# Each engine gets its own order of head steps in both layers, and the first layer's tail of y ends in the next pair

## The chip, the cores and the metric

The program runs on one core of a Trainium2 chip. That core has five engines that work side by side and meet only at semaphores: TensorE (PE, matrix products and transposes into PSUM), VectorE (DVE), ScalarE (ACT), GpSimd (POOL) and SyncE (SP, which here only issues DMA transfers). Each engine takes its own instructions strictly in the order in which they are written. An instruction whose semaphore is not there yet holds up everything behind it on its engine. The metric is the device time of one execution in microseconds (us).

## The reference, cut to what matters

```python
x = L0_attn_x                                    # (8, 256, 128)
for layer in (0, 1):
    xn = _layernorm(x)
    s = attn(xn)      # a selective scan over 256 tokens; 16 states (layer 0) or 2 x 16 chunks (layer 1)
    g = _silu(ffn(xn))  # 8 experts, 128 -> 512 -> 128; layer 0: one-hot choice, layer 1: a soft mixture
    x = x + s * g
# in attn, per state n:   h = exp(delta * A[n]) * h + delta * B[n] * xs;   y += h * C[n]
# layer 0 ends with       y = layernorm(y + x_res) * gamma + beta;  s = y @ W_out.T + b_out
# layer 1 ends with       y = (y + xs * Dskip) * silu(z);           s = y @ out_proj.T
```

All is fp32. The eight sequences are worked in four pairs (512 tokens each), all four through the first layer and then all four through the second, with the result of the first in a DRAM tensor `x1`.

## The kernel before

**Slots.** The work of a pair in a layer is written in 32 slots (`UNITS`), one for each of the 8 x 4 tiles of the experts' hidden layer. Every engine has its own function `slot0` (first layer) or `slot1` (second layer), which is called once per slot. So what stands in slot 7 on DVE and on PE is a statement about order, not about time: an engine that runs ahead is in a later slot than another at the same moment.

**A first-layer slot.** PE makes a hidden tile in three passes (L1413 to L1415, `three_passes`), ACT rectifies it (L1217), and PE multiplies the one of two slots ago by the down weights (L1470). Next to that run the 16 scan chunks, at the slots of `CHUNKS0` (0, 1, 2, 4, 5, 7, 8, 9, 11, 12, 14, 15, 16, 18, 19, 21): ACT makes the decay (L1204), DVE the drive (L652, from a row of B and C that a DMA spreads over the partitions into a ring of four tiles `CB`) and, a slot later, the scan (L659), POOL multiplies by C and adds up (L940 to L948), and PE sums groups of four into `Y_BANK` (L1434).

**A second-layer slot.** There are 32 chunks, almost one a slot, and PE has a gate tile (in pairs: the gates of two tiles in one slot), an up product (L1529) and a down product (L1538). There is one PSUM bank for the up product. `up` of a tile waits until DVE has multiplied the tile before it into `hid` (L775), and DVE waits for the up product. This ties PE and DVE together within about a slot.

**The head.** Before a pair's slots can start, its head has to be done: layer norm (`stat1`, `var1`, `xn`), the transpose `xnT`, the input products (`xin`, or `xi0`, `xi1`, `z0`, `z1`), the router (`logits`, `lmax`, `lexp`, then `pick`, `onehot` or `soft1` to `soft3`, `cwT`), the convolution (`tap1` to `tap3`, `xs`), the rows of B and C (`row`), and softplus (`dt`, `rest`, `less`, `ln`). The head of the next pair is spread over slots 6 (`LATE`) to 31 of the pair before. One table (`HEAD0` at L63, `HEAD1` at L66) says in which slot a step stands, **for all engines at once**. A step that needs several engines (`dt`: PE multiplies, ACT applies softplus) stands in the same slot on each. Nearly all head products go through one PSUM bank, `HEAD_BANK`. PE may write the next one only when the last has been read (`head_read`).

**The end of a pair.** In the first layer `TAIL0` (L85) closes y: add and transpose y in slot 27, its layer norm in 28 to 30, `ynT` and the product `s` in 31, all on the pair's own slots. What is left of the feed-forward result is in `late0`, in slots 0 to 5 of the next pair. DVE selects the last expert in slot 2, PE transposes into the head bank in slot 3 (L1517, L1518), ACT applies tanh in slot 3 (L1246), DVE multiplies in slots 4 and 5 (L718, L724), and POOL adds the residual (L979). The second layer has `late1` for the same: DVE adds y in slot 2 (L781), PE has both the transposes and the output product in slot 3, ACT tanh in 3 (L1289), DVE in 4 and 5.

**The queue of SP.** The DMAs stand in one program too. `send_rows` and `send_mask` write to DRAM and wait for the landing, and the loads of `CB` rows stand behind them.

## Time and profile before

| | before |
|---|---|
| median of 3 runs | 908.33 us (901.88 to 913.71) |
| the profiled execution | 906.77 us, of which 904.7 us are the span from first to last instruction |
| mean granted TensorE clock | 0.943 of full speed |
| busy: PE, DVE, ACT, POOL | 738.9, 631.9, 506.3, 527.0 us (82%, 70%, 56%, 58%) |
| longest waits of PE in total | 56.8 us in 44 waits of the up product for DVE's `hid`; 27.4 us in 4 waits of a transpose for DVE's `xn` |
| longest wait of ACT in total | 124.5 us in 87 waits for PE before a rectification |

No engine is full. One that waits is, most of the time, waiting in its own fixed order for something that another engine has in a later place of its own. A row of the timeline reads: start in us, length, engine, line, operation, out<-in, count, and in brackets the idle time of the engine before it with what ended it.

### The profile page before, as it was taken

How to read it: one execution, taken by the hardware profiler on the slowest of the kernel's cores; microseconds unless marked ns; L12 is line 12 of the kernel's file. 1: busy time of each engine (PE TensorE's matmuls, PEld its weight loads, DVE VectorE, ACT ScalarE, POOL GpSimd, SP SyncE). 2: the span in 40 equal slices, each digit the busy share in tenths (PEclk: the TensorE clock that was granted, in tenths of full speed). 3: DMA queues.
4: the chain of work that ended last, by engine and by line, in shares of the span. 5: the costliest groups of instructions: out<-in, count | busy, mean ns of one | idle time of the engine just before them, and what ended most of it. 6: DMA issues, size and time to landing. Idle time of an engine off the chain costs nothing. (4 is left out here: it accounts for less than half of the span.)

```text
span 904.7 us, 8892 instructions
## 1 busy us (share of the span) xinstructions
PE 738.9 (82%) x2160; PEld 392.1 (43%) x2160; DVE 631.9 (70%) x1013; ACT 506.3 (56%) x755; POOL 527.0 (58%) x420
## 2 busy tenths in 40 slices
PE   2747987899789967868799769898778896888996
PEld 1324554455445543434444335453344442344443
DVE  4399559936984765357776578766669676778884
ACT  2734544455446535676646557557557456656661
POOL 0086526534661563208856658866659765659894
PEclk9988988998899989989999999999889999999999
DMA  9275465443734583267735467747456655648881
GB/s 269 74 214 153 124 221 144 137 140 98 181 97 132 153 227 90 76 155 185 200 106 150 123 161 182 190 124 175 119 146 179 183 143 124 152 125 214 203 192 34
DMA packets 90515, 137.86 MB, mean 152 GB/s; under 512 B 7896, under 2 KB 29088, under 8 KB 90464
## 3 DMA queue, kind: packets, MB, share of 16 engines
q1 hardware_dynamic: 90464, 137.30, 57.1%
q8 instruction: 17, 0.28, 0.1%
q14 instruction: 34, 0.28, 0.1%
HBM read 133.73 MB, written 3.54 MB: 152 GB/s over the span
## 5 line engine op out<-in xcount | busy, mean ns | idle before, releaser
L659 DVE TENSOR_TENSOR_SCAN state<-decay,bank 128x512 f32<-128x512 f32 x192 | 233.7, 1217 | 11.7 <-ACT decay L1204 1.0
L1413 PE MATMUL bank<-XH,wh 128*128 128x512 f32 x256 | 170.9, 667 | 26.7 <-ACT sg L1253 12.8
L1529 PE MATMUL bank<-xw,wu 128*128 128x512 f32 x256 | 141.5, 635 | 57.1 <-DVE hid L775 56.8
L923 POOL TENSOR_TENSOR product<-state,CB 128x512 f32<-128x512 f32 x96 | 122.4, 1275 | 86.4 <-DVE state L659 84.6
L1217 ACT ACTIVATE hid<-bank,early 128x512 f32<-128x512 f32 x128 | 86.9, 684 | 132.7 <-PE bank L1470 124.5
L652 DVE TENSOR_TENSOR bank<-bank,CB 128x512 f32<-128x512 f32 x192 | 133.5, 695 | 27.9 <-DMA CB<-crow 20.7
L1470 PE MATMUL bank<-hid,wd 128*128 128x512 f32 x256 | 143.6, 644 | 0.0
L1204 ACT ACTIVATE decay<-delta,negA 128x510 f32<-128x510 f32 x192 | 126.9, 710 | 10.0 <-DVE delta L639 7.3
L1538 PE MATMUL bank<-hid,wd 128*128 128x512 f32 x256 | 132.2, 599 | 0.0
L925 POOL TENSOR_TENSOR product<-product 128x512 f32<-128x512 f32 x96 | 123.6, 1288 | 7.5
L1253 ACT ACTIVATE sg<-bank 128x512 f32<-128x512 f32 x128 | 74.3, 597 | 89.2 <-PE bank L1415 81.0
L775 DVE TENSOR_TENSOR hid<-sg,bank 128x512 f32<-128x512 f32 x128 | 85.9, 671 | 54.0 <-PE bank L1529 49.3
L1414 PE MATMUL bank<-XL,wh 128*128 128x512 f32 x256 | 107.2, 419 | 0.0
L1415 PE MATMUL bank<-XH,wl 128*128 128x512 f32 x256 | 106.8, 417 | 0.0
L1529 PEld LDWEIGHTS bank<-xw,wu 128*128 128x128 f32 x256 | 44.5, 194 | 139.4 <-DVE hid L775 85.9
L944 POOL TENSOR_TENSOR product<-state,CB 128x512 f32<-128x512 f32 x48 | 61.4, 1280 | 72.0 <-DVE state L659 69.8
L1413 PEld LDWEIGHTS bank<-XH,wh 128*128 128x128 f32 x256 | 51.9, 203 | 88.0 <-issue 37.2
L1414 PEld LDWEIGHTS bank<-XL,wh 128*128 128x128 f32 x256 | 52.2, 204 | 38.4 <-issue 35.1
L948 POOL TENSOR_TENSOR product<-product 128x512 f32<-128x512 f32 x48 | 62.8, 1307 | 3.8
L1538 PEld LDWEIGHTS bank<-hid,wd 128*128 128x128 f32 x256 | 47.9, 191 | 37.0 <-issue 30.7
L992 POOL TENSOR_TENSOR xw<-XR,cwb 128x512 f32<-128x512 f32 x32 | 42.1, 1316 | 30.5 <-DVE wl L529 13.7
L919 POOL TENSOR_TENSOR product<-state,CB 128x512 f32<-128x512 f32 x32 | 40.9, 1277 | 31.1 <-DVE state L659 17.8
(166 smaller groups left out, 922.3 us busy)
## 6 DMA issues: line engine op xcount, KB each, us to landing
CB<-crow SPq DMA_DIRECT2D x256, 256.0 KB, 5.1
CB<-crow SPq DMA_DIRECT2D x64, 512.0 KB, 5.4
cwb<-cwrow SPq DMA_DIRECT2D x64, 256.0 KB, 5.6
wu<-W_dram SPq DMA_DIRECT2D x8, 256.0 KB, 5.9
wd<-W_dram SPq DMA_DIRECT2D x8, 256.0 KB, 5.9
wu<-Wu_dram SPq DMA_DIRECT2D x8, 256.0 KB, 5.6
xw<-Wg_dram SPq DMA_DIRECT2D x8, 256.0 KB, 4.1
wd<-Wd_dram SPq DMA_DIRECT2D x8, 256.0 KB, 4.3
```

The costliest lines, as they stand in the source:

```text
L652: v.tensor_tensor(drive, dx, CB[:, c % ROWS, 1, :], ALU.mult).then_inc(drive_ready.sem, 1)
L659: v.tensor_tensor_scan(state[:, c % RING, :], decay[:, PLACE[c], :], drive, 0.0, ALU.mult, ALU.add).then_inc(state_ready.sem, 1)
L923: p.tensor_tensor(addend, state[:, c % RING, :], cs, ALU.mult).then_inc(state_used.sem, 1)
L925: ins = p.tensor_tensor(product[:, e % PRODS, :], product[:, e % PRODS, :], addend, ALU.add)
L1204: a.activation(by_batch(decay[:, PLACE[c], :])[:, :, 1:], by_batch(delta[:, m, :])[:, :, 1:], ACT.Exp, scale=negA[:, c:c + 1]).then_inc(de ...
L1217: a.activation(hid[:, u % 2, :], bank[HID_BANK + u % HIDS][:, :], ACT.Relu, bias=col0("b1", u)).then_inc(hid_ready.sem, 1)
L1413: t.matmul(dst, wh[:, e, ws], XH[:, :], start=True, stop=False)
L1414: t.matmul(dst, wh[:, e, ws], XL[:, :], start=False, stop=False)
L1415: return t.matmul(dst, wl[:, e, ws], XH[:, :], start=False, stop=stop)
L1470: t.matmul(bank[out_bank(e)][:, :], wd[:, u, :], hid[:, u % 2, :], start=(f == 0), stop=(f == FT - 1)).then_inc(down_done.sem, 1)
L1529: t.matmul(bank[UP_BANK][:, :], wu[:, e, 128 * f:128 * f + 128], xw[:, e % 2, :], start=True, stop=True).then_inc(up_ps.sem, 1)
L1538: ins = t.matmul(bank[OUT_BANK][:, :], wd[:, u, :], hid[:, u % 2, :], start=(u == 0), stop=(u == UNITS - 1))
```

## The change

**Own orders.** For the heads that run beside another pair of the same layer, the common tables give way to one table per engine: `PE0`, `ACT0`, `DVE0`, `POOL0` for the first layer and `PE1`, `ACT1`, `DVE1`, `POOL1` for the second. A reader of something stands a slot or more behind its maker in nearly all places (in the second layer PE's `dt0` stands in slot 17, and it needs the head bank free of `cwT`, which ACT reads in slot 17 too). The heads start at slot 1 instead of 6: DVE has `xn` in slot 4 where it was in 9, PE has `xnT` in 7 where it was in 11. The loads of x move ahead for that. `HEAD0` and `HEAD1` remain for the very first head and for the head of the second layer's first pair, which runs in the last pair of the first layer. Their numbers change too: the `z0`, `z1` steps move from 16 and 20 to 23 and 25, and `onehot` goes to the end of the first head.

```diff
-HEAD0 = {6: "stat1", 7: "var1", 9: "xn", 10: "stat2", 11: "xnT var2", 12: "xin", 13: "logits xf tap1", 14: "lmax tap2",
+PE0 = {7: "xnT", 9: "xin", 11: "logits", 13: "xfT", 15: "z", 18: "dt", 20: "row", 22: "onehot"}
+DVE0 = {1: "stat1", 2: "var1", 4: "xn", 5: "stat2", 7: "var2", 9: "xf", 11: "tap1", 12: "lmax tap2", 13: "tap3", 14: "prob",
+        15: "pick", 16: "xs", 17: "zx", 22: "rest"}
+EXTRA = {3: "xi0", 4: "xi1", 5: "z0", 6: "z1"}
+PE1 = {6: "xnT", 8: "logits", 9: "xi0a", 10: "xi0b", 13: "row0 xi1a", 14: "xi1b", 15: "cwT", 17: "dt0", 18: "z0",
+       21: "row1", 22: "z1", 23: "dt1"}
...
-FINISH_Y0 = CHUNKS1[N - 1] + SUM_LAG1
-
-TAIL0 = {27: "y", 28: "yn1", 29: "yn2", 30: "yn", 31: "ynT s"}
+FINISH_Y0 = CHUNKS1[N - 1] + SUM_LAG1 + 1
+
+DVE_TAIL0 = {27: "y", 29: "yn1 yn2", 31: "yn"}
+PE_TAIL0 = {28: "y"}
+DVE_LATE0 = {1: "ynT", 3: "s"}
+PE_LATE0 = {0: "yn", 2: "s"}
...
+STREAM = [item for e in range(E) for item in ([EXTRA[e]] if e in EXTRA else []) + list(range(FT * e, FT * e + FT))]
+def stream_bank(item):
+
+    return HID_BANK + STREAM.index(item) % HIDS
...
+            def gate_at(i):
+
+                return 4 if i == PAIRS - 1 else 6
...
-                v.tensor_scalar(ynT, dx, col0("gam"), col0("bet"), ALU.mult, ALU.add).then_inc(ynT_ready.sem, 1)
+                    v.tensor_scalar(ynT, bank[Y_BANK][:, :], col0("gam"), col0("bet"), ALU.mult, ALU.add).then_inc(ynT_ready.sem, 1)
...
-                if u == 2:
+                if u == 3:
                     finish_y(i, 1)
 
-                if u == 4:
+                if u == 5:
                     dve.wait_ge(tg_ready.sem, tg_ready.at1(i, 1))
...
+            load_x(1, 0)
+            send_rows(0, 0, 0)
             send_mask(0)
-            send_rows(0, 0, 0)
```

**The extras of the second layer.** `xi0`, `xi1`, `z0`, `z1` no longer pass through the head bank. Each takes a place in the stream of gate tiles through the two `HID` banks, ahead of expert 3, 4, 5, 6. ACT reads it just before the four gate tiles of that expert. Round these places PE writes one gate tile in one slot and three in the next, where it was two and two. The four products of `xi` are written in two halves.

**The tails.** In the first layer the transposes of yn, `ynT`, and the product `s` move to slots 0 to 3 of the next pair, and go through `Y_BANK` alone. DVE's two steps of the gate move from slots 4 and 5 to 6 and 7 (`gate_at`), in another buffer. In the second layer DVE adds the end of y in slot 3 instead of 2. The output product and tanh are in slot 4 instead of 3, DVE's product in 5 instead of 4.

On DVE, in the first layer, at the start of the second pair, before: `L718` is the first step of the gate of the pair before (`yfT`), `L724` the second.

```order
L652 TENSOR_TENSOR bank<-bank,CB 128x512
L659 SCALAR_TENSOR_TENSOR state<-decay,bank 128x512
L718 SCALAR_TENSOR_TENSOR yfT<-yfT,bank 128x512
L652 TENSOR_TENSOR bank<-bank,CB 128x512
L659 SCALAR_TENSOR_TENSOR state<-decay,bank 128x512
L724 SCALAR_TENSOR_TENSOR so<-yfT,hp,so 128x128 x4
L652 TENSOR_TENSOR bank<-bank,CB 128x512
L659 SCALAR_TENSOR_TENSOR state<-decay,bank 128x512
L631 MEMSET pause 128x1
L632 COPY_PREDICATED yfT<-cwb,bank 128x512
L682 COPY szm<-ohT 8x512
```

The same place now, from the third scan on. `L782` and `L788` are the gate's two steps, `L602` is `xn` of the next pair, `L738` the end of `s`.

```order
L714 SCALAR_TENSOR_TENSOR state<-decay,bank 128x512
L738 TENSOR_TENSOR so<-bank,bout 128x512
L707 TENSOR_TENSOR bank<-bank,CB 128x512
L602 TENSOR_SCALAR xn<-xt,mv,rstd 128x128 x4
L714 SCALAR_TENSOR_TENSOR state<-decay,bank 128x512
L707 TENSOR_TENSOR bank<-bank,CB 128x512
L589 BN_STATS stats<-xn 128x6 x4
L714 SCALAR_TENSOR_TENSOR state<-decay,bank 128x512
L782 SCALAR_TENSOR_TENSOR sg<-sg,bank 128x512
L686 MEMSET pause 128x1
L687 COPY_PREDICATED yfT<-cwb,bank 128x512
L788 SCALAR_TENSOR_TENSOR so<-sg,hp,so 128x128 x4
```

The gate moved behind two more scans, and `xn` of the next pair now stands ahead of it.

On DVE, in the second layer, at the start of the second pair, before: `L781` adds the end of y, which needs the last sum of PE, and the scan of the new pair stands behind it.

```order
L659 SCALAR_TENSOR_TENSOR state<-decay,bank 128x512
L652 TENSOR_TENSOR bank<-bank,CB 128x512
L781 TENSOR_TENSOR xd<-xd,bank 128x512
L785 TENSOR_TENSOR xd<-xd,szm 128x512
L659 SCALAR_TENSOR_TENSOR state<-decay,bank 128x512
L775 TENSOR_TENSOR hid<-sg,bank 128x512
```

Now, where the same two steps are `L845` and `L849`:

```order
L714 SCALAR_TENSOR_TENSOR state<-decay,bank 128x512
L839 TENSOR_TENSOR hid<-sg,bank 128x512
L707 TENSOR_TENSOR bank<-bank,CB 128x512
L593 MEMSET idle 128x1
L595 BN_AGGR mv<-stats 128x2 x4
L597 TENSOR_SCALAR veps<-mv 128x4
L845 TENSOR_TENSOR xd<-xd,bank 128x512
L849 TENSOR_TENSOR xd<-xd,szm 128x512
L714 SCALAR_TENSOR_TENSOR state<-decay,bank 128x512
```

The end of y moved one scan and one `hid` back.

On ACT, in the second layer, where the router's weights `cwT` and softplus of `dt0` stand now (second pair, slots 16 to 19): `L1206` is the extra, `L1319` are four gate tiles, `L1267` four decays, `L1222` is `cwT`, `L1146` on is `dt0`.

```order
L1206 ACT_TABLE_LOAD
L1206 ACTIVATE xs<-bank,early 128x512
L1319 ACTIVATE sg<-bank 128x512 x4
L1267 ACT_TABLE_LOAD
L1267 ACTIVATE decay<-delta,negA 128x2x255 x4
L1222 ACTIVATE ohT<-bank 8x512
L1146 ACTIVATE sp_e<-bank,early 128x512
L1147 ACTIVATE sp_x<-bank,early 128x512
```

Before, `cwT` (L1159) was the last of these steps, behind both softplus steps:

```order
L1253 ACTIVATE sg<-bank 128x512 x4
L1204 ACT_TABLE_LOAD
L1204 ACTIVATE decay<-delta,negA 128x2x255 x4
L1083 ACTIVATE sp_e<-bank,early 128x512
L1084 ACTIVATE sp_x<-bank,early 128x512
L1085 ACTIVATE sp_e<-sp_e 128x512
L1087 ACTIVATE sp_u<-sp_e 128x512
L1159 ACTIVATE ohT<-bank 8x512
```

`cwT` moved from behind the second softplus to ahead of the first.

## Rows read from the trace of the kernel before

**Rows 1.** Busy time by pair: stretch, length, PE, PEld, DVE, ACT, POOL, PEclk, DMA share, GB/s

```profile
27.50:121.20 93.70, 71.77 (x218) 40.24 (x217) 66.94 (x121) 51.98 (x82) 45.88 (x37) 0.93 0.56 169
121.20:206.30 85.10, 72.41 (x229) 42.19 (x228) 62.45 (x119) 43.52 (x70) 42.01 (x33) 0.90 0.49 136
291.40:395.00 103.60, 80.80 (x247) 44.54 (x246) 57.01 (x103) 58.78 (x95) 41.39 (x33) 0.92 0.47 130
395.00:527.80 132.80, 112.60 (x310) 55.93 (x308) 93.80 (x131) 79.06 (x115) 87.75 (x69) 0.95 0.63 164
527.80:656.80 129.00, 109.66 (x312) 55.38 (x312) 93.99 (x130) 79.21 (x114) 89.26 (x70) 0.96 0.61 152
```

**Rows 2.** Timeline of PE in the first layer's second pair: rows with a wait

```profile
153.03 1.09 PE L1338 MATMUL bank<-early,xn 128*128 128x128 f32 x4 [5.48 <-DVE xn L547]
...
165.72 0.66 PE L1338 MATMUL bank<-early,sg 128*128 128x128 f32 x4 [1.56 <-DVE lg L592]
...
173.66 0.58 PE L1367 MATMUL bank<-early,onehot 128*8 128x128 f32 x2 [2.60 <-DVE onehot L599]
```

**Rows 3.** Timeline of DVE, first layer: the gate's wait, and xn there and at the start

```profile
134.33 0.69 DVE L718 SCALAR_TENSOR_TENSOR yfT<-yfT,bank 128x512 f32<-128x512 f32 x1 [5.92 <-ACT yfT L1246]
...
149.81 3.08 DVE L547 TENSOR_SCALAR xn<-xt,mv,rstd 128x128 f32<-128x128 f32 x4
```

**Rows 4.** Timeline of DVE at the very start, with POOL idle

```profile
9.54 1.12 DVE L547 TENSOR_SCALAR xn<-xt,mv,rstd 128x128 f32<-128x128 f32 x4 [4.54 <-POOL rstd L890]
```

**Rows 5.** Busy time of the second pair up to DVE's zx (columns as in rows 1)

```profile
121.20:180.90 59.70, 48.70 (x148) 28.54 (x147) 51.32 (x91) 28.84 (x48) 34.60 (x27) 0.86 0.51 139
```

**Rows 6.** The page's costliest groups: DVE's scan and drive

```profile
L659 DVE TENSOR_TENSOR_SCAN state<-decay,bank 128x512 f32<-128x512 f32 x192 | 233.7, 1217 | 11.7 <-ACT decay L1204 1.0
...
L652 DVE TENSOR_TENSOR bank<-bank,CB 128x512 f32<-128x512 f32 x192 | 133.5, 695 | 27.9 <-DMA CB<-crow 20.7
```

**Rows 7.** Timeline of PE in the first layer's last pair: rows with a wait

```profile
323.46 1.09 PE L1338 MATMUL bank<-early,xn 128*128 128x128 f32 x4 [7.24 <-ACT xn L1132]
...
343.32 1.19 PE L1343 MATMUL bank<-XNP,later 128*128 128x512 f32 x2 [3.59 <-ACT xs L1143]
...
394.21 1.16 PE L1494 MATMUL bank<-later,xd 128*128 128x128 f32 x8 [3.97 <-DVE xd L703]
```

**Rows 8.** Timeline of PE in the second layer's second pair: rows with a wait

```profile
541.05 1.13 PE L1529 MATMUL bank<-xw,wu 128*128 128x512 f32 x2 [3.76 <-DVE hid L775]
...
577.34 0.50 PE L1413 MATMUL bank<-XH,wh 128*128 128x512 f32 x1 [2.60 <-ACT sg L1253]
...
618.24 1.13 PE L1529 MATMUL bank<-xw,wu 128*128 128x512 f32 x2 [1.45 <-DVE hid L775]
...
625.86 0.50 PE L1413 MATMUL bank<-XH,wh 128*128 128x512 f32 x1 [1.27 <-ACT sg L1253]
...
637.38 2.07 PE L1529 MATMUL bank<-xw,wu 128*128 128x512 f32 x2 [4.05 <-DVE hid L775]
...
652.59 1.12 PE L1529 MATMUL bank<-xw,wu 128*128 128x512 f32 x2 [1.84 <-DVE hid L775]
```

**Rows 9.** Timeline of ACT and DVE there: what these waits hang on

```profile
574.78 0.60 ACT L1138 ACTIVATE XNP<-bank 128x512 f32<-128x512 f32 x1 [5.58 <-PE bank L1338]
...
634.92 0.69 DVE L563 SCALAR_TENSOR_TENSOR sp_e<-sp_u,sp_e 128x512 f32<-128x512 f32 x1 [4.34 <-ACT sp_u L1087]
```

**Rows 10.** Busy time round the longest wait and round the pair's start

```profile
626.00:640.00 14.00, 9.93 (x21) 4.11 (x22) 8.20 (x11) 7.85 (x12) 9.16 (x8) 0.80 0.59 125
524.40:546.10 21.70, 15.54 (x47) 8.98 (x47) 15.43 (x18) 9.81 (x15) 11.96 (x10) 0.92 0.53 138
```

**Rows 11.** Timeline of ACT and SP at the start: before the first CB rows

```profile
39.49 0.20 ACT L1115 ACTIVATE warm<-ones 128x1 f32<-128x1 f32 x1
...
38.07 2.87 SPq L371 DMA_DIRECT2D CB<-crow  x4
```

**Rows 12.** Waits of SP's queue: total, times, longest

```profile
SPq L412 <- ACT ohT L1159: 41.2, 4, 11.5
```

336 lines of the change are left out of this document (199 added, 137 removed).

## Prediction

> **What bounds the kernel now.** First the busy time by pair [rows 1]. The reader sees two kinds of pairs. A first-layer pair takes 85.1 us, in which PE is busy for 72.4 and DVE for 62.5. The first pair takes 93.7, the third is like the second, and the last takes 103.6, since it carries the second layer's head. A second-layer pair with a head beside it takes 129.0 to 132.8 us, with PE at 110 to 113, DVE at 94 and POOL at 88 to 89. PE is thus nearest to a bound in both layers, but 12.7 us of the first kind and 19.3 us of the second are idle on PE. Its work does not change, so what can be won is this idle time, and what the clock loses round it (granted 0.90 and 0.96).
>
> Then the timeline of PE, only the rows that have a wait. In the first layer a pair has three that count: 5.48 us for `xn`, 1.56 for the router's `lmax`, 2.60 for `onehot` [rows 2]. All are head steps, where PE stands in the same slot as, or close behind, a DVE step that is late. DVE is late because it sat still itself for 5.92 us, for ACT's tanh of the old pair's gate, before its fourth scan [rows 3]. In the second layer there are the 3.76 us at the pair's start and then 2.60, 1.45, 1.27, 4.05 and 1.84, together 11.2 [rows 8]. ACT and DVE show what stands behind two of them: ACT waits 5.58 us for `xnT` with four gate tiles queued behind it, and DVE waits 4.34 us in `rest1` for ACT's softplus with the scan and the next `hid` queued behind [rows 9]. Both are waits of a reader that stands in its maker's slot.
>
> **The change, first layer.** No instruction is added but for the split of `xi`, and no pass is removed. The sum is one of places. Take a middle pair (85.1 us) in two parts.
>
> Up to `zx`, which the next `dt` product of PE waits for, DVE should set the pace: the old stretch is 59.7 us long with 51.3 of DVE work [rows 5], so 8.4 idle. In the new order `zx` stands in slot 17 and no more in 20. Two scans (1.22 each), two drives (0.70 each) and a select (taken as a drive) now come after it [rows 6], 4.5 us less. `ynT` and `s` come in from the pair before, at about a drive each, 1.4 us more. That leaves 48.2 us of work. The 5.92 us wait falls: the gate is behind two more scans and PE's transposes, which ACT waits for, are long done. `xn` for PE's slot 7 is made in DVE's slot 4. I put 2 us for what DVE still waits (short gaps of dependent instructions), so `dt` can start some 50 us into the pair. Before it PE will wait anew: by this count DVE needs more than PE for slots 8 to 12, so about 4 us for `lmax` (PE slot 13, DVE slot 12) and 2 us for `zx`. These waits are in the 50.
>
> From there to the end PE sets the pace. The old stretch from `onehot` (slot 18, at 173.66) to the pair's end at 206.3 is 32.6 us [rows 1, 2]. `z` leaves it (1.2 us, by the like product) and so does `s` (1.2 us) [rows 7]. Some 1.5 us more go, because the clock stays up with the 2.60 us wait gone and because the yn transposes no longer wait in slot 31. That makes 28.7. The pair takes 79 us, 6 less. Twice: 12.
>
> Here price and place of `xn` matter. At 149.81 its four pieces took 3.08 us beside POOL's products [rows 3], at the very start, with POOL idle, 1.12 us [rows 4]. In slot 4 POOL has chunk 2 in hand, so I keep 3.08; `xf` is the same form. The Trainium skill (SBUF — State Buffer, Who interferes with whom) says why: VectorE and GpSimd share one pair of SBUF ports as an exclusive lock, and whoever comes second blocks for the whole instruction. By the start's row both steps together would cost 4 us less and the pair 75; by that rule, as by the row beside POOL, 79.
>
> The first pair gains the same kind of waits, but pays at the start. `CB` rows could be loaded from 38.07 on, once the rows of B and C were out. Now `send_mask` stands ahead of the loads, and its `onehot` is copied by ACT behind the warm-up at 39.49 [rows 11]. Bounds: 1.6 us if the rest hides, about 5 with the copy and a landed write; a shorter first head gives back about one. I take 3 later. Gain 6 less 3: 3 us.
>
> The last first-layer pair: 7.24 us for `xn`, 3.59 for `xs0` ahead of `z0`, 3.97 for `ynT` ahead of `s` [rows 7], 14.8 in all. `xnT` stays in slot 11, but DVE no longer sits 5.9 us before it; 5 of 7.2 fall. The `z` wait falls, since z is now 7 slots behind `xs0`; a new one of about 2 us comes in slot 24, where `row1` needs the bank that ACT reads only after softplus. `ynT` is gone from this place. 5 + 3.6 - 2 + 3.4 = 10.
>
> First layer: 3 + 12 + 10 = 25 us.
>
> **The change, second layer.** At a pair's start, DVE's end of y needs PE's last sum, and the scan stands behind it. One slot later it should find the sum ready: the 3.76 us fall. The stretch round it ran at 0.92 of the clock [rows 10], 1.7 us lost at 21.7 us, of which I count 1.4. So 5.2 at each of three starts.
>
> In the slots of a head: the five waits of 11.2 us fall as they stand, and so does a loss of clock (0.80 over 14 us with PE busy 9.9 [rows 10]), 2 us. In their place come new ones. (a) PE's `dt0` in slot 17 needs `cwT` read by ACT in slot 17, and there ACT has an extra, four gate tiles, a table load and four decays ahead of it. (b) Three gate tiles in one slot instead of two, four times: the third waits for ACT. (c) `xs1` waits for DVE's `dx` of slot 15, and a gate tile waits for `xs1`. (d) SP's three blocking sends now lie within slots 14 to 22. No row shows these waits. Below they cost nothing; above, I bound them by the 11.2 us that they replace. I take 7, nearer to the upper end, since (a) is exactly the pattern of what is removed, and (b) to (d) are of one or two us each. So a head stretch gains 11.2 + 2 - 7 = 6.2. First pair: 6.2, less the 1.2 us of `s`, the waits of the first layer's tail in its slots 0 to 5, and a smaller loss of clock: 3. Second and third: 6.2 + 5.2 = 11.4 each. Last: 5.2. Second layer: 31 us.
>
> **Sum.** 906.8 - 25 - 31 = 851 us, against the profiled execution's own 906.77. That is 1.6 us below the median of the runs, 908.33, so I leave it as it is.
>
> **Rivals.** (1) The new waits are small: nothing in the second layer's (a) to (d), and DVE's and PE's parts of a first-layer pair overlap better. 21 us back there, some 6 in the first layer: about 824 us. For it speaks that the waits left on PE would then be those of the ties between `up` and `hid`.
> (2) The waits only move, half. DVE fills the first layer (62.5 of then 79 us), and its head steps meet POOL more often, each for up to 2 us more [rows 3, 4]; in the second layer (a) to (d) cost all of the 11.2. 4 x 3 + 3 x 4.2 + some 2: 878 us. The port lock of the Trainium skill is the rule that speaks for this.
> (3) The waits move one for one: PE and DVE are tied within a slot, and what is taken from one slot is waited for in the next. Only the starts (3 x 3.8) stay won: 895 us. Against it: the removed waits have a named cause, a reader in its maker's slot.
> (4) Slower: SP's queue. The `CB` loads stand behind `row0`, `cwT`, `row1`, now in slots 14, 17 and 22. A wait of SP for ACT's `cwT` reached 11.5 us [rows 12]. If each of the nine held the scans for 9 us, 81 us would be lost against 56 won: about 932 us. It decides from (56 + 18) / 9 = 8.2 us each. Against it: the ring holds four rows, and DVE waited for `CB` only 20.7 us over the whole run [rows 6].
>
> **How the numbers follow.** The forecast (836 to 868) 0.52; (1) 0.12; (2) 0.17; (3) 0.14; (4) 0.05. The predicted time is that of the forecast. The range 818 to 886 takes in the forecast, (1) and (2), 0.81. A measurement of this kernel, whose three runs lie 1.3% apart, can tell about 2% (890 us) from no change. Faster by over 2%: 0.81; within 2%: 0.14; slower: 0.05.
>
> **What would show it.** In the changed profile: first-layer middle pairs of 77 to 81 us. DVE's gate step without an idle time ahead of it, and `xnT` with less than 2 us. PE waits for `lmax` and for `zx` that are longer than before. Second-layer pairs of 116 to 119 us, no wait over 2 us in the up product at the start, and a wait of about 2 us before `dt0`. `CB` rows first loaded at about 41 us. The prediction is wrong if DVE waits for `CB` rows for far more than 20.7 us, if DVE's `xn` or `xf` takes over 3.1 us, or if PE's idle time in a second-layer pair stays above 16 us.

## The result, and the profile after

The changed kernel took 851.6 us (median of 4 runs, 845.5 to 853.8) beside 906.0 us (901.9 to 913.7) of the kernel before: a ratio of 0.938, 95% interval 0.930 to 0.947. The forecast was 851 us with a range of 818 to 886. The total was met almost to the microsecond, but not because each term was: several were wrong by 2 to 11 us and cancelled. The rest of this text is about that.

| | after |
|---|---|
| the profiled execution | 845.54 us, span 843.1 us |
| mean granted TensorE clock | 0.965 |
| busy: PE, DVE, ACT, POOL | 722.5, 618.1, 507.6, 531.0 us (86%, 73%, 60%, 63%) |
| longest waits of PE in total | 27.2 us (was 56.8) of the up product for DVE's `hid` |
| longest wait of ACT in total | 110.8 us (was 124.5) before a rectification |

The busy time by pair of the changed kernel answers [rows 1]. Columns: stretch, length, PE, PEld, DVE, ACT, POOL, PEclk, DMA share, GB/s.

```profile
27.50:120.50 93.00, 73.91 (x214) 40.68 (x214) 64.61 (x119) 52.12 (x83) 46.82 (x37) 0.89 0.57 168
120.50:196.60 76.10, 65.65 (x229) 38.35 (x228) 60.49 (x119) 42.87 (x70) 42.76 (x33) 1.00 0.54 151
196.60:272.90 76.30, 68.89 (x230) 40.19 (x229) 60.73 (x119) 43.13 (x71) 42.78 (x33) 0.96 0.52 149
272.90:373.70 100.80, 82.31 (x253) 46.23 (x252) 56.30 (x108) 62.39 (x98) 42.70 (x34) 0.92 0.51 144
373.70:490.70 117.00, 105.99 (x305) 53.19 (x305) 90.42 (x130) 79.53 (x116) 85.59 (x68) 0.98 0.68 176
490.70:610.80 120.10, 110.25 (x313) 55.08 (x312) 92.33 (x129) 79.28 (x113) 89.55 (x71) 0.97 0.65 167
610.80:729.80 119.00, 108.74 (x313) 53.96 (x312) 92.76 (x129) 79.27 (x114) 89.59 (x71) 0.99 0.63 166
729.80:843.10 113.30, 99.04 (x291) 49.96 (x289) 88.56 (x110) 61.78 (x84) 88.95 (x70) 1.00 0.64 159
sum 815.60, PE 714.78 PEld 377.63 DVE 606.21 ACT 500.38 POOL 528.74; mean PE 89.35 PEld 47.20 DVE 75.78 ACT 62.55 POOL 66.09
```

The cuts are at ACT's first rectification or Silu of a pair. Read at the same marks, the kernel before has pairs of 93.6, 85.2, 85.1, 107.0, 131.1, 128.9, 130.6 and 115.8 us (its fourth pair is longer here than in [rows 1], whose cuts lay a little earlier). So the eight pairs gained 0.7, 9.0, 8.9, 6.2, 14.0, 8.8, 11.6 and 2.5 us: 24.8 in the first layer (forecast 25) and 36.9 in the second (forecast 31).

What of this is idle time and what is clock? The same sum for the kernel before, by layer:

```profile
27.60:398.40 370.80, 300.96 (x925) 170.83 (x925) 251.45 (x463) 199.04 (x316) 172.23 (x137) 0.91 0.51 143
398.40:904.70 506.30, 429.07 (x1211) 215.70 (x1210) 368.48 (x493) 299.29 (x425) 352.51 (x278) 0.97 0.61 156
```

PE was idle for 877.1 - 730.0 = 147.1 us of this and is now idle for 815.6 - 714.8 = 100.8: 46.3 us less. In the other 15.2 us PE is busy for less: the same products in less time, at a higher granted clock (0.94 and 0.98 of full by layer, 0.91 and 0.97 before; 5.1 of the 15.2 lie in the second layer).

The two waits that the prediction expected to grow in a first-layer pair are the first two rows of the timeline of PE (second pair); the next two are the places foreseen in the second layer (sixth pair):

```profile
154.56 0.66 PE L1398 MATMUL bank<-early,sg 128*128 128x128 f32 x4 [3.80 <-DVE lg L647]
...
167.60 0.70 PE L1403 MATMUL bank<-xs,early 128*128 128x512 f32 x1 [2.87 <-DVE xs L670]
...
507.04 1.49 PE L1635 MATMUL bank<-xw,wu 128*128 128x512 f32 x2 [1.92 <-DVE hid L839]
...
562.78 1.12 PE L1403 MATMUL bank<-rows,w_dt 32*128 32x512 f32 x2 [1.34 <-ACT ohT L1222]
...
599.40 0.50 PE L1505 MATMUL bank<-XH,wh 128*128 128x512 f32 x1 [2.22 <-ACT sg L1319]
```

`lmax` 3.80 us (forecast 4), `zx` 2.87 (forecast 2), the longest wait at the start of the sixth pair 1.92 (forecast: none over 2), and `dt0` 1.34 (forecast 2). The last one, 2.22 us before a gate tile, was in no list.

And DVE up to `zx`, where the prediction said that it sets the pace (columns as above; the second row is the rest of the pair):

```profile
120.50:167.50 47.00, 38.34 (x138) 22.57 (x136) 45.31 (x88) 26.47 (x45) 31.70 (x25) 1.00 0.61 169
167.50:196.60 29.10, 27.31 (x91) 15.78 (x92) 15.18 (x34) 16.41 (x25) 11.07 (x9) 1.00 0.42 122
```

DVE works 45.3 of 47.0 us. The stretch was forecast at some 50, the rest at 28.7.

Cut at the start of `zx` itself, and not behind it, the same two parts can be read in every kernel, also in those of the experiments below. "Clock" is the granted clock, "2" and "3" the second and third pair (us):

```text
kernel and pair      up to zx  clock    rest  clock
before, 2                59.1   0.86    26.0   1.00
after, 2                 46.4   1.00    29.7   1.00
after, 3                 46.5   0.93    29.8   1.00
after, again, 3          46.4   0.93    31.3   0.95
cb_first, 2              46.4   0.93    32.7   0.90
gate_early, 2            50.6   0.87    29.8   1.00
gate_early, 3            49.7   0.90    29.8   1.00
tail_in_pair, 2          47.4   0.89    32.9   0.95
tail_in_pair, 3          46.0   0.93    32.7   0.95
head0_old, 2             53.0   0.97    23.4   1.00
same_slot0, 2            44.3   0.96    30.6   1.00
```

Up to `zx` the length does not follow the clock: 46.4 us at 1.00 and at 0.93. Behind it, it does: 29.7 us at 1.00, 31.3 at 0.95, 32.7 at 0.90 (the edit of `cb_first` does not touch this pair). That bears out the prediction's two parts, DVE's and then PE's. It also shows that the 12.7 us won ahead of `zx` are not the clock's: with the gate undone the stretch ran at 0.87, nearly as low as before, and took 50.6 us, not 59.1. Four of these rows as the profile gives them (`gate_early`, `tail_in_pair`, `cb_first`, the second execution):

```profile
121.30:171.90 50.60, 41.92 (x138) 25.09 (x136) 45.48 (x85) 25.38 (x43) 31.12 (x24) 0.87 0.58 155
...
171.30:204.20 32.90, 30.15 (x99) 17.52 (x100) 16.89 (x37) 16.44 (x26) 11.30 (x10) 0.95 0.36 111
...
162.90:195.60 32.70, 30.26 (x91) 17.37 (x92) 14.97 (x35) 16.40 (x25) 11.32 (x10) 0.90 0.38 113
...
244.10:275.40 31.30, 28.92 (x91) 16.64 (x92) 15.64 (x35) 16.44 (x26) 11.25 (x10) 0.95 0.43 126
```

### The profile page after: what moved, and what is told of

It is laid out like the page before. It is cut to its first block and busy times, and to the rows that moved or that the text cites. A ratio compares the mean times of both kernels' runs of the same rounds, so it can differ in the third digit from the quotient of the medians.

```text
span 843.1 us, 8895 instructions
## 1 busy us (share of the span) xinstructions
PE 722.5 (86%) x2160; PEld 382.7 (45%) x2160; DVE 618.1 (73%) x1013; ACT 507.6 (60%) x757; POOL 531.0 (63%) x420
## 5 line engine op out<-in xcount | busy, mean ns | idle before, releaser
L714 DVE TENSOR_TENSOR_SCAN state<-decay,bank 128x512 f32<-128x512 f32 x192 | 233.7, 1217 | 11.3 <-ACT decay L1267 0.9
L1505 PE MATMUL bank<-XH,wh 128*128 128x512 f32 x256 | 172.3, 673 | 26.3 <-ACT hid L1280 10.9
L1635 PE MATMUL bank<-xw,wu 128*128 128x512 f32 x256 | 137.6, 619 | 27.5 <-DVE hid L839 27.2
L1280 ACT ACTIVATE hid<-bank,early 128x512 f32<-128x512 f32 x128 | 86.9, 684 | 119.8 <-PE bank L1568 110.8
L707 DVE TENSOR_TENSOR bank<-bank,CB 128x512 f32<-128x512 f32 x192 | 133.4, 695 | 26.4 <-DMA CB<-crow 18.9
L1319 ACT ACTIVATE sg<-bank 128x512 f32<-128x512 f32 x128 | 75.4, 597 | 104.3 <-PE bank L1507 94.7
L839 DVE TENSOR_TENSOR hid<-sg,bank 128x512 f32<-128x512 f32 x128 | 85.9, 671 | 64.8 <-PE bank L1635 61.5
L1267 ACT ACTIVATE decay<-delta,negA 128x510 f32<-128x510 f32 x192 | 126.9, 710 | 8.0 <-DVE state L714 4.5
L987 POOL TENSOR_TENSOR product<-product 128x512 f32<-128x512 f32 x96 | 124.2, 1293 | 7.5
L1506 PE MATMUL bank<-XL,wh 128*128 128x512 f32 x256 | 105.1, 411 | 0.0
L1010 POOL TENSOR_TENSOR product<-product 128x512 f32<-128x512 f32 x48 | 65.0, 1354 | 3.8
L1057 POOL TENSOR_TENSOR xw<-XR,cwb 128x512 f32<-128x512 f32 x32 | 42.1, 1315 | 25.1 <-DMA cwb<-cwrow 20.7
```

What stands on the lines that cost most here:

```text
L707: v.tensor_tensor(drive, dx, CB[:, c % ROWS, 1, :], ALU.mult).then_inc(drive_ready.sem, 1)
L714: v.tensor_tensor_scan(state[:, c % RING, :], decay[:, PLACE[c], :], drive, 0.0, ALU.mult, ALU.add).then_inc(state_ready.sem, 1)
L987: ins = p.tensor_tensor(product[:, e % PRODS, :], product[:, e % PRODS, :], addend, ALU.add)
L1267: a.activation(by_batch(decay[:, PLACE[c], :])[:, :, 1:], by_batch(delta[:, m, :])[:, :, 1:], ACT.Exp, scale=negA[:, c:c + 1]).then_inc(de ...
L1280: a.activation(hid[:, u % 2, :], bank[HID_BANK + u % HIDS][:, :], ACT.Relu, bias=col0("b1", u)).then_inc(hid_ready.sem, 1)
L1505: t.matmul(dst, wh[:, e, ws], XH[:, :], start=True, stop=False)
```

## The experiments

All start from the changed kernel. Most were timed once only, and one time differs from the next by up to 1%, so the verdicts rest on the length of pairs in the trace, cut at the same marks. This table has them all (us):

```text
pair                   1      2      3      4      5      6      7      8    span
before               93.6   85.2   85.1  107.0  131.1  128.9  130.6  115.8   904.7
after                92.9   76.2   76.2  100.8  117.0  120.1  119.0  113.3   843.1
after, again         93.9   76.2   77.7  102.1  116.8  120.1  119.3  114.6   848.4
gate_early           93.8   80.4   79.4  105.7  116.8  122.8  120.1  114.9   861.3
tail_in_pair         96.4   80.3   78.7  101.6  119.8  119.1  119.0  114.7   857.1
head0_old            93.9   76.4   76.2  100.8  120.8  120.4  118.9  115.0   849.8
same_slot0           93.3   75.0   74.9  102.0  120.0  120.1  119.5  114.6   846.9
same_slot1           93.1   76.2   76.2  100.8  122.7  126.2  126.9  113.3   862.9
l2_start             93.4   76.2   77.6  102.0  117.3  122.5  122.3  119.4   858.4
cb_first             89.0   79.1   76.2   99.0  117.5  119.2  119.2  114.7   841.3
tail_first           94.1   76.2   76.2   94.5  123.1  120.6  118.8  115.2   846.2
tail_cb1             93.8   76.2   76.2   95.0  118.8  120.3  118.7  112.9   839.3
two_steps            94.2   76.2   76.2  100.8  117.9  119.8  118.7  114.6   846.0
together             87.8   74.9   74.9   97.8  117.7  119.2  122.9  115.1   837.9
```

### How sharp a pair is

> The changed kernel as it is, once more, to see how far the length of a pair differs between two profiled executions of one program. If a pair is a sharp measure, the eight lengths are 92.9, 76.2, 76.2, 100.8, 117.0, 120.1, 119.0 and 113.3 us again, each within 0.5 us. If the clock's low stretches fall at other places each time, single pairs differ by 1 to 3 us, and only sums of several pairs can be read.

No edit. It took 850.3 us. Single pairs differ by up to 1.5 us, and PE's idle time over all pairs was 100.7 against 100.8 us. In the second layer it repeats pair by pair, within 0.4 us. In the first it repeats only in sum: the first pair had 2.1 us more of it, the second 3.0 less, and the second was as long as before. So a difference under 1.5 us in one pair is no verdict, unless it returns in others. The fifth pair is the worst mark: it was 3.0 to 4.0 us longer in two kernels whose edits cannot reach it (same_slot0, head0_old) while its idle time was 11.3 and 10.5 us, as in the changed kernel (11.0).

### The gate step back in slot 4

```diff
         def gate_at(i):
-            return 4 if i == PAIRS - 1 else 6
+            return 4
```

> The gate step of the pair before is back in slot 4 for every pair, where it was; the head steps and the tail of y keep their new places. Theory of the prediction: VectorE's wait of 5.9 us for ScalarE's tanh was what made the head of the next pair late, so moving it removes most of a middle pair's gain. The wait comes back with 4 to 6 us, and the second and third pair take 80 to 82 us instead of 76.2; the other pairs stay. Rival: the gain comes from the early start of the head's statistics (slots 1 to 5), and the gate step has slack in either place. Then the wait comes back, but the pairs take at most 77.5 us.

863.3 us. The timeline of DVE (the gate) and of PE (the product behind `lmax`) in the second pair:

```profile
135.14 0.69 DVE L782 SCALAR_TENSOR_TENSOR sg<-sg,bank 128x512 f32<-128x512 f32 x1 [3.56 <-ACT sg L1312]
...
159.59 1.12 PE L1398 MATMUL bank<-early,sg 128*128 128x128 f32 x4 [7.03 <-DVE lg L647]
```

In the changed kernel the gate step stands at 137.37 with no idle time ahead of it, and PE waits 3.80 (2.81 in the second execution). Here DVE waits 3.56 us, PE's wait grows to 7.03 us, and the second, third and fourth pair take 4.2, 1.7 to 3.2 and 3.6 to 4.9 us more (the fourth holds the gate of the third). The whole of it lies ahead of `zx`, where the clock does not count: 50.6 and 49.7 us instead of 46.4 in the second and third pair, and the rest is unchanged. The theory holds, a little below its size: 3.2 to 4.2 of a middle pair's 9 us hang on one instruction's slot, on the engine that sets the pace.

### The tail of y back in its own pair

```diff
-DVE_TAIL0 = {27: "y", 29: "yn1 yn2", 31: "yn"}
-PE_TAIL0 = {28: "y"}
-DVE_LATE0 = {1: "ynT", 3: "s"}
-PE_LATE0 = {0: "yn", 2: "s"}
+DVE_TAIL0 = {27: "y", 28: "yn1", 29: "yn2", 30: "yn", 31: "ynT s"}
+PE_TAIL0 = {27: "y", 30: "yn", 31: "s"}
+DVE_LATE0 = {}
+PE_LATE0 = {}
```

> The tail of y of a first-layer pair (slots 27 to 31 on VectorE and TensorE) ends again within the pair; the head steps and the gate keep their new places. Theory of the prediction: the tail cost a middle pair 1.4 us of VectorE's slots either way, and at the last first-layer pair 3.4 us of waiting in slot 31. So the second and third pair stay within 1 us of 76.2 (77.7 at most, by the clock's stretches), and the fourth takes 3 to 4 us more than 100.8 to 102.1. Rival: the tail in the pair is a chain TensorE, VectorE, TensorE, VectorE in five slots whose waits stop both engines in every pair. Then the second and third pair take 3 us or more longer too.

858.9 us. Here the prediction's own account fell on both counts. The first pair takes 2.5 to 3.5 us more, the second 4.0, the third 1.0 to 2.5; the fourth, where it saw 3.4 us, is unchanged. What the tail takes in a middle pair is seen in DVE's waits at the boundary:

```profile
190.24 0.69 DVE L722 TENSOR_TENSOR xd<-XR,bank 128x512 f32<-128x512 f32 x1 [1.58 <-PE bank L1526]
...
193.41 0.89 DVE L589 BATCH_NORM_STATS2 stats<-bank 128x6 f32<-128x128 f32 x4 [2.49 <-PE bank L1398]
...
196.62 0.06 DVE L686 MEMSET pause<- 128x1 f32 x1 [1.69 <-PE bank L1568]
...
201.82 0.69 DVE L738 TENSOR_TENSOR so<-bank,bout 128x512 f32<-128x512 f32 x1 [1.65 <-PE bank L1581]
```

These are turns between DVE and PE, one after the other, and the next pair's first scan stands behind them on DVE. In the changed kernel the waits of 4.0 us before the statistics and 1.6 before `y` are as long or longer, but `ynT` and `s` no longer stand between the pair's end and the next scan. At the last first-layer pair PE's waits become 4.76 us for `y`, 0.62 for `yn` and 3.97 for `s` (as [rows 7]), 9.4 together, where the changed kernel has 3.20 and 5.62, 8.8 together: the tail costs about the same there in both orders.

Not all of the 4.0 and 2.5 us is the tail's. Behind `zx` the two pairs take 32.9 and 32.7 us, 3 more than in the changed kernel, but at a granted clock of 0.95, and a pair with the new tail took 31.3 there at the same clock. So with the clock taken off, the tail costs 2.6 us in the second pair and 1.0 in the third. Whether its waits also bring the lower clock is not shown.

### The first layer's head in its old slots

```diff
+HEAD0 = {6: "stat1", 7: "var1", 9: "xn", 10: "stat2", 11: "xnT var2", 12: "xin", 13: "logits xf tap1", 14: "lmax tap2",
+         15: "lexp xfT tap3", 16: "th pick", 17: "xs prob", 18: "onehot", 19: "z", 20: "zx", 22: "dt", 23: "row", 24: "rest",
+         25: "less ln"}
+PE0 = ACT0 = DVE0 = POOL0 = HEAD0
...
-FIRST = steps(HEAD0)[:steps(HEAD0).index("z")]
-BETWEEN = {0: "z zx", 1: "dt", 2: "row rest", 3: "less ln onehot"}
+FIRST = steps(HEAD0)[:steps(HEAD0).index("onehot") + 1]
+BETWEEN = {0: "z zx", 1: "dt", 2: "row rest", 3: "less ln"}
...
+            send_mask(0)
             send_rows(0, 0, 0)
-            send_mask(0)
...
-                    if u == LATE and i + 2 < PAIRS:
+                    if u == LATE + 4 and i + 2 < PAIRS:
                         load_x(i + 2, 0)
```

> The first layer's head has its old slots and one order for all engines (xnT 11, onehot 18, z 19, dt 22), also ahead of the first pair; gate step and tail of y keep their new places. A middle pair went from 85.1 to 76.2 us. Putting the gate back alone gave 79.4 and 80.4, the tail alone 78.7 and 80.3. Theory: the three parts add up, and the early head is worth what is left, 1.5 to 3 us, so the second and third pair take 78 to 80 us. Rival A: the head's new places carry most of the gain (the waits for lmax, xs and onehot), and the pairs take 81 to 84 us. Rival B: gate and tail matter only because the early head needs the slots that they left; with the old head their new places are enough by themselves, and the pairs take under 77.5 us.

851.9 us, and the second and third pair take 76.4 and 76.2 us, as with the new tables. Rival B is right. With the gate and the tail in their new places, `PE0`, `ACT0`, `DVE0` and `POOL0` add nothing to a middle pair. No run takes gate and tail back together, so it is not shown that these two make the whole 9 us. The old `xn` wait, 5.48 us in [rows 2], is down to 1.80 without the head having moved, since DVE does not sit still before it. Timeline of PE, second pair:

```profile
146.89 0.63 PE L1394 MATMUL bank<-early,xn 128*128 128x128 f32 x4 [1.80 <-DVE xn L598]
...
159.83 0.66 PE L1394 MATMUL bank<-early,sg 128*128 128x128 f32 x4 [3.44 <-DVE lg L643]
```

The sum shows why the places don't matter. Here `zx` comes at 174.4, in slot 20, and the stretch from 121.4 to 174.0 is 52.6 us long with 49.4 of DVE work. In the changed kernel `zx` starts 46.4 us into the pair, here 53.0. But PE has the one-hot behind it by then, and the rest of the pair is 23.5 us here and 29.8 there. What leaves DVE's part joins PE's.

The first pair is another matter. This kernel issues its first rows at 38.17 us, as early as the kernel before (38.07), and still takes 93.9 us there, while a kernel with the new tables and the rows at 37.40 takes 89.0 (`cb_first`, below). So in that pair up to 4.9 us hang on the new tables or on the new order of the very first head. The two were not tried apart.

### Readers a slot earlier, first layer

```diff
-ACT0 = {8: "xnT", 10: "xin", 13: "lexp", 14: "xfT th", 19: "dt", 21: "row", 23: "onehot", 24: "ln"}
-DVE0 = {..., 11: "tap1", 12: "lmax tap2", 13: "tap3", 14: "prob", 15: "pick", 16: "xs", 17: "zx", 22: "rest"}
-POOL0 = {2: "var1", 7: "var2", 23: "less"}
+ACT0 = {7: "xnT", 9: "xin", 12: "lexp", 13: "xfT th", 18: "dt", 20: "row", 22: "onehot", 23: "ln"}
+DVE0 = {..., 10: "tap1", 11: "lmax tap2", 12: "tap3", 13: "prob", 14: "pick", 15: "xs zx", 20: "rest"}
+POOL0 = {2: "var1", 7: "var2", 20: "less"}
```

> First layer only, TensorE's places as changed, but every reader of a head product (ScalarE's copies, dt, row, one-hot, VectorE's lmax and zx) and VectorE's steps of the chain to it stand one slot earlier, most in TensorE's own slot. Theory: a reader in its maker's slot waits for it with the next hidden unit queued behind, so ScalarE's and VectorE's waits for head products rise from under 1 us to 2 us or more each, and the second and third pair take 79 to 83 us instead of 76.2 to 77.7. Rival: in the first layer it is only the early start of the head and the late gate that matter, and a reader in its maker's slot waits about as long as TensorE needs for one product (0.6 us). Then these pairs take at most 78 us, and may be shorter, since TensorE's waits for lmax (2.8 us) and for xs (1.3 us) begin to shrink when VectorE's steps come a slot earlier.

848.9 us. The second and third pair take 75.0 and 74.9 us, 1.2 less than with the readers a slot behind. The rival holds: `zx` starts 44.3 us into the pair and not 46.4, since DVE reaches it with less ahead of it. In this layer the rule "a reader a slot behind its maker" is at best worth nothing. ACT is busy for 42.9 of 76.1 us in such a pair of the changed kernel, and PE hardly waits for it: 0.9 us there, 1.8 here. ACT itself does wait in the maker's slot, 1.9 us for `dt`, and the pair is shorter all the same.

### Readers in their maker's slot, second layer

```diff
-ACT1 = {5: "xn", 7: "xnT", 10: "lexp", 14: "row0", 17: "cwT", 19: "dt0", 22: "row1", 25: "dt1", 27: "ln", ...
-DVE1 = {..., 9: "lmax", ..., 21: "rest0", 26: "rest1", ...
-POOL1 = {2: "var1", 21: "less0", 27: "less1"}
+ACT1 = {5: "xn", 6: "xnT", 9: "lexp", 13: "row0", 16: "cwT", 17: "dt0", 21: "row1", 24: "dt1", 27: "ln", ...
+DVE1 = {..., 8: "lmax", ..., 18: "rest0", 25: "rest1", ...
+POOL1 = {2: "var1", 18: "less0", 25: "less1"}
```

> Second layer only, TensorE's places as changed, but ScalarE's and VectorE's readers of the head products stand in TensorE's own slot (xnT 6, lmax 8, row0 13, dt0 17, row1 21) or as near as the order of the bank lets them (cwT 16, dt1 24), and the rest steps one slot behind. Theory: each reader in its maker's slot stops ScalarE with four gate tiles behind it, or VectorE with a scan and a hid behind it, as in the kernel before, where these waits were 4.05, 1.84 and 1.45 us. The fifth, sixth and seventh pair take 4 to 8 us more each than 117.0, 120.1 and 119.2. Rival: the gain came from taking xi and z out of the head's one bank into the stream of gate tiles; a slot of distance is worth little. Then these pairs stay within 2 us.

864.9 us: 5.7, 6.1 and 7.6 to 7.9 us more in the three pairs with a head. The theory holds here. PE's idle time is 15.2, 14.1 and 14.4 us instead of 11.0, 9.8 and 10.3, and the largest piece is the old pattern of [rows 8] and [rows 9]. Timeline of DVE and PE, sixth pair:

```profile
602.25 0.69 DVE L618 SCALAR_TENSOR_TENSOR sp_e<-sp_u,sp_e 128x512 f32<-128x512 f32 x1 [3.95 <-ACT sp_u L1150]
602.86 1.21 DVE L714 TENSOR_TENSOR_SCAN state<-decay,bank 128x512 f32<-128x512 f32 x1
603.99 0.66 DVE L839 TENSOR_TENSOR hid<-sg,bank 128x512 f32<-128x512 f32 x1
...
604.71 2.07 PE L1635 MATMUL bank<-xw,wu 128*128 128x512 f32 x2 [4.91 <-DVE hid L839]
```

DVE waits 3.95 us for softplus; a scan and the next `hid` are queued behind; PE waits 4.91 for that `hid`, and its up product takes 2.07 us instead of 1.12: the granted clock was 1.00 when this wait began and is 0.50 in the product (1.2 and no more 2.4 GHz). In the three pairs 4.2, 4.3 and 4.1 us of the loss are idle time of PE; the other 1.5 to 3.8 are its products at a lower clock (0.95 to 0.96 instead of 0.97 to 0.99). Note that `rest1` did stand a slot behind its maker. ACT's `dt1` was in slot 24, where four gate tiles and the decays come first. Distance is counted in the maker's work, not in slots.

### The end of y at a second-layer start

```diff
-                if u == 3:
+                if u == 2:
                     finish_y(i, 1)
```

> Only VectorE's end of y (second half) goes back from slot 3 to slot 2 of the next second-layer pair. Theory of the prediction: this one slot is worth 3.76 us of PE's time at each of three starts, and about 1.4 us of clock with it. So the 6th, 7th and 8th pair take 3.5 to 5 us longer each (from 120.1, 119.0 and 113.3 us), and the span is 10 to 15 us longer, 853 to 858 us. Rival: the wait for the last sum moved on to the other waits at the start (1.9 and 0.9 us stand there now), or was made by head steps beside it that are gone. Then the wait before the up product comes back with at most 2 us, and the span is longer by at most 5 us.

860.2 us. The wait is back exactly where it was, in each of three starts. Timeline of PE, seventh and eighth pair:

```profile
630.36 2.08 PE L1635 MATMUL bank<-xw,wu 128*128 128x512 f32 x2 [3.75 <-DVE hid L839]
...
752.70 2.07 PE L1635 MATMUL bank<-xw,wu 128*128 128x512 f32 x2 [3.76 <-DVE hid L839]
```

The three pairs take 2.4, 3.1 and 5 to 6 us more. The place is right; the price in the sixth and seventh is not 5.2 but about 3, since the waits of 0.61, 1.92 and 0.92 us of the changed kernel's start are gone in turn (PE's idle time: 11.5 and 11.1 us instead of 9.8 and 10.3; the rest is a granted clock of 0.96 instead of 0.97 and 0.99).

### The start's rows of B and C first

```diff
             send_rows(0, 0, 0)
+            for c in range(ROWS):
+                load_cb0(0, c)
             send_mask(0)
...
-                for c in range(ROWS):
+                for c in range(ROWS if i else 0):
                     load_cb0(i, c)
```

> SyncE loads the first four rows of B and C before it waits for the one-hot mask, as the kernel before did. Theory of the prediction: the mask ahead of these loads costs the first pair 3 us, so it falls from 92.9 to about 90 us, the rows are issued at about 38 us and no more at 41.5, and VectorE's wait of 6.1 us before its first drive halves. Rival: the first pair has its time from another engine, and the loads only end one wait of a chain. Then the drive's wait is shorter, and the pair stays within 0.5 us of 92.9. All later pairs as they are in both.

843.4 us. Queue of SP and drives of DVE at the start, this kernel and then the changed one (second execution):

```profile
37.40 2.74 SPq L421 DMA_DIRECT2D CB<-crow  x4
...
42.40 0.70 DVE L709 TENSOR_TENSOR bank<-bank,CB 128x512 f32<-128x512 f32 x1 [1.93 <-DMA CB<-crow]
```

```profile
41.51 2.74 SPq L421 DMA_DIRECT2D CB<-crow  x4
...
46.44 0.70 DVE L707 TENSOR_TENSOR bank<-bank,CB 128x512 f32<-128x512 f32 x1 [6.01 <-DMA CB<-crow]
```

The rows are issued 4.1 us earlier, and the first pair is 3.9 to 4.9 us shorter, as its first drive is 4.1 us earlier. That fits a first pair which hangs on this drive. (The expectation is wrong on the kernel before. It too sent the mask ahead of these loads, but as early as 24.58 us, when nothing had to wait for it.) The second pair, though, took 79.1 us: its granted clock was 0.91 (1.00 in the changed kernel), with PE busy for 71.6 us and idle for 7.5. Its part up to `zx` is as long as ever, 46.4 us. All of the 3 us lie behind it, where the clock counts.

### y and yn ahead of the weights' low half

```diff
+                for name in now(DVE_TAIL0, u):
+                    tail(i, name)
                 if head is head1 and u % FT == FT - 1 and u // FT >= 1:
                     split_low(E + u // FT - 1)
-                for name in now(DVE_TAIL0, u):
-                    tail(i, name)
```

> In the last first-layer pair VectorE does y and yn ahead of the low half of the second layer's weights in the same slot (27 and 31), and no more behind it. In the changed kernel TensorE waits there 3.20 us for y and 5.62 us for yn, while VectorE stands at the weights' low half, which waits for ScalarE's high half behind softplus and its table loads. Theory: only the order on VectorE makes these waits. Both fall to 1 us or less, and the fourth pair takes 95 to 97 us instead of 100.8 to 102.1 (99.0 with the earlier loads). Rival: y and yn wait for their own makers (the last sum, the square root on GpSimd) or the weights' low half is then late for its reader. Then one of the two waits stays above 2 us or a new one of that size stands before the second layer's first gate tiles, and the pair takes at least 99 us. All other pairs as they are.

848.2 us. This is the reason for the last first-layer pair. In the changed kernel PE and DVE have (timelines of both):

```profile
356.96 0.66 PE L1398 MATMUL bank<-early,xd 128*128 128x128 f32 x4 [3.20 <-DVE xd L722]
...
369.52 0.69 PE L1398 MATMUL bank<-early,so 128*128 128x128 f32 x2 [5.62 <-DVE so L602]
...
355.61 0.69 DVE L584 TENSOR_TENSOR wl<-xw,wh 128x512 fp32r<-128x512 f32 x1 [8.28 <-ACT wh L1133]
356.22 0.68 DVE L722 TENSOR_TENSOR xd<-XR,bank 128x512 f32<-128x512 f32 x1
...
367.49 0.69 DVE L584 TENSOR_TENSOR wl<-xw,wh 128x512 fp32r<-128x512 f32 x1 [3.01 <-ACT wh L1133]
368.10 1.36 DVE L602 TENSOR_SCALAR so<-bank,mv,rstd_t 128x128 f32<-128x128 f32 x4
```

`y` and `yn` stand right behind a split of weights that waits 8.28 and 3.01 us for ACT. With the two lines exchanged, the 3.20 is gone, the 5.62 is 2.11, a new wait of 2.43 us (a gate tile for DVE's `XL`) stands behind them, and the fourth pair takes 94.5 us, 6.3 to 7.6 less. But the fifth takes 123.1: together 217.6 us, against 217.8 and 218.9. The order on DVE is the cause of the two waits, and curing it alone brings nothing, because the next start then has to wait:

```profile
370.74 0.70 DVE L707 TENSOR_TENSOR bank<-bank,CB 128x512 f32<-128x512 f32 x1 [2.16 <-issue]
...
374.52 0.70 DVE L707 TENSOR_TENSOR bank<-bank,CB 128x512 f32<-128x512 f32 x1 [1.24 <-DMA CB<-crow]
...
378.49 1.65 PE L1635 MATMUL bank<-xw,wu 128*128 128x512 f32 x2 [3.73 <-DVE hid L839]
```

The first drives want the second layer's rows of B and C. The trace has no event for the end of the first idle time ("issue"), so that it too ends with these rows was a guess, which the next run tests.

### The same, with the second layer's rows earlier

```diff
+                    if last and u == 29:
+                        for c in range(ROWS):
+                            load_cb1(0, c)
...
-                for c in range(ROWS):
+                for c in range(ROWS if i else 0):
                     load_cb1(i, c)
```

> The kernel with y and yn ahead of the weights' low half, and beside it the first four rows of B and C of the second layer issued in slot 29 of the last first-layer pair and no more behind its last weights and x. With the order on VectorE alone the fourth pair took 94.5 us and the fifth 123.1, in sum 217.6 against 217.8 and 218.9 of the changed kernel: the gain was given back, while VectorE's first two drives of the second layer waited 2.2 and 1.2 us for these rows. Theory: the rows were next in the chain, so the fourth pair stays at 94 to 95 and the fifth falls to 119 to 121, in sum 213.5 to 215.5. Rival: the fifth pair's start is bound by something else as well (the mask's row for GpSimd, or the gate of the first layer's last pair, for which VectorE waited 4.5 us). Then the two drive waits go and the sum stays above 216.5.

841.4 us. The fourth and fifth pair take 95.0 and 118.8, in sum 213.7, as the theory says. The first two drives now start at 368.76 and 371.43 with less than 0.1 us of idle time ahead of them. The rows had stood in SP's queue behind slot 31's weights and x.

### Two steps in the second layer

```diff
-PE1 = {..., 15: "cwT", 17: "dt0", 18: "z0", ...
+PE1 = {..., 15: "cwT", 18: "dt0 z0", ...
-ACT1 = {..., 25: "dt1", 27: "ln", ...
+ACT1 = {..., 25: "dt1", 28: "ln", ...
```

> Second layer, two steps moved by one slot: TensorE's dt0 from 17 to 18, ahead of z0, and ScalarE's ln from 27 to 28, behind the four gate tiles. Theory: the first is a reader of the bank that ScalarE frees only in slot 17 behind an extra tile, four gate tiles and four decays, so TensorE's wait of 1.34 us goes in each of three pairs; the second stands with two table loads ahead of the Silu load of the last four gate tiles and makes TensorE's 2.22 us wait, which goes too. The fifth, sixth and seventh pair take 2 to 3.5 us less than 117.0, 120.1 and 119.2. Rival: these waits lie in front of others, and ln is then late for the next pair's delta and first scan. The two waits go from their places, waits of the same size stand in slots 29 to 3, and the pairs change by less than 1 us.

848.0 us. Both waits go from their places, and others come, in the sixth pair:

```profile
572.04 0.50 PE L1505 MATMUL bank<-XH,wh 128*128 128x512 f32 x1 [1.12 <-ACT sz L1218]
...
608.48 2.07 PE L1635 MATMUL bank<-xw,wu 128*128 128x512 f32 x2 [2.98 <-DVE hid L839]
```

1.34 and 2.22 us became 1.12 and 2.98. PE's idle time is 10.9 us instead of 9.8. The rival holds: this is the case "one for one" of the prediction's third rival. It is true of what is left now, as it was not true of what the change removed.

### What helped, together

The edits of cb_first, tail_cb1 and same_slot0 in one kernel.

> Three edits that helped alone, in one kernel: the start's rows of B and C ahead of the mask; y and yn ahead of the weights' low half together with the second layer's first rows from slot 29; and the first layer's readers a slot earlier. Alone they brought the first pair 4 to 5 us (88.98 against 92.9 to 93.9), the fourth and fifth pair together 4 to 5 us (213.7 against 217.8 to 218.9), and the second and third pair 1.3 us each. The clock's low stretches move by some 3 us from run to run. Theory: the three lie in different pairs and add up to 11 us, so the span is 832 to 837 us and the time about 836 to 841 (ratio 0.92 to 0.93 to the kernel before, where the changed kernel has 0.938). Rival: each gain sets the clock low at another place, or is given back at the next boundary of pairs, as the second pair's 79.1 us behind the faster first pair suggests. Then the span is 839 us or more, no better than the best part alone.

838.4 us (median of 6, 834.3 to 845.1), a ratio of 0.924 to the kernel before, 95% interval 0.920 to 0.929, beside 0.938 (0.930 to 0.947) of the changed kernel. The intervals just touch; every one of its six times lies below every one of the changed kernel's four in the first measurement. PE's idle time is 96.4 us, 4.4 less. The span of 837.9 us is 1 to 6 above the sum of the parts: the first three pairs have their full gain, the fourth and fifth together take 215.5 us (213.7 with their edit alone), while the seventh took 122.9 us with the granted clock at 0.96 and idle time of 11.0, where it had 119.0, 0.99 and 10.3. Against the best edit alone (`tail_cb1`, one time of 841.4 us) the kernel is not clearly faster: two of its own six times lie near that or above it.

## Why the prediction was right, point by point

The mechanism was right in the main: PE's idle time was to fall, and 46.3 of the 61.5 us are idle time. That the sum came out at 851 is luck. The profiled execution, from which the terms are read, is the fastest of the four: 845.5 us, 5 below the forecast (the second one took 850.3). The terms missed by 2.3, 3.0, 2.9, 3.8, 11.0, 2.6, 0.2 and 2.7 us from the first to the eighth pair, half of them too high and half too low.

**The first pair: forecast 3, measured 0.7 (second execution: none).** The step on SP's queue was right in place and under-sized: 3 us was taken between 1.6 and 5, and undoing it brought 3.9 to 4.9. The gain beside it, put at 6 as in a middle pair, is 93.6 less 89.0: 4.6. Here the new tables may well be what brings it (93.9 with the old head).

**The middle pairs: forecast 6 each, measured 9.0 and 8.9.** The account was right where it said what happens: DVE sets the pace up to `zx` and waits for little, the gate's wait falls, PE's waits for `lmax` and `zx` grow. The rest after `zx` was forecast at 28.7 us and took 29.1. The stretch before it took 3 us less than the 50. That is the price of two instructions. `xn` and `xf` were taken at 3.08 each beside POOL's products; they took 2.19 and 1.10. By the start's 1.12 us for both the pair would have been 75; it came out at 76.2. The forecast let the new place of `zx` win 4.5 us in DVE's part and lengthen PE's from 25.4 to 28.7, some 1 us net; the run with the old head shows that it is a shift and no gain at all, 76.4 and 76.2 us. What wins is the rest of the forecast's DVE part, the waits that it let fall. But only parts of it have a price. The gate's slot is worth 3.2 to 4.2 us when undone, and the tail's 1.0 to 2.6 (up to 4.0 with a lower clock). The forecast had named the gate; it had put nothing down for the tail's waits in a middle pair, only 1.4 us of DVE's work, the same in either order. That leaves 2 to 5 of the 9 us not assigned. `xn` and `xf` may be in it, but that is not shown: with the old head they took 1.10 and 3.14, a microsecond more together, in a pair of the same length.

That the middle pairs came out at 76.2 and not at 79 is in part luck. The price of `xn` and `xf` was known to lie between 1.12 and 3.08, and PE's part is as short as 29.8 us only at the full clock. At 0.90 there (`cb_first`) it is 32.7, and the pair takes 79.1.

**The last first-layer pair: forecast 10, measured 6.2 (4.9 the second time).** The `z0` wait fell (3.6, right), and the new one before `row1` was 1.51 us (forecast 2). The `xnT` wait fell from 7.24 to 4.64, 2.6 and not 5. The failing step is the tail: "`ynT` is gone from this place", 3.4 us. 3.97 us went, but y's wait rose from 2.68 to 3.20 and one of 5.62 came for `yn`. The prediction looked at where `ynT` went and not at what `yn` would now stand behind, a split that waits for ACT.

**The second layer's starts: forecast 5.2 each.** Right in place and cause, too large: 2.4 and 3.1 us in the sixth and seventh pair, 5 to 6 in the eighth. In the eighth pair PE's idle time tells it best: 17.2 us before, 14.2 after, 17.6 with the step undone. That is 3.0 to 3.4 us for the wait of 3.76. Whether the 1.4 us of clock came with it is open. From before to after it did not: PE was busy for 98.6 us and then 99.0, so the pair gained only 2.5 us. With the step undone PE was busy for 101.8 us at a granted clock of 0.97, against 99.0 at 1.00 and 100.4 at 0.99 in the two executions of the changed kernel.

**The head's slots: new waits forecast at 7 us.** In the sixth pair they are 1.34 for (a), and for (b) to (d) nothing that was foreseen; 2.22 before a gate tile, made by `ln` and its two table loads, came in their place, and 1.5 us in three pieces of the up product. About 5 us, for 11.2 removed. (c) is in the trace, a wait of ACT up to 4.4 us for DVE's `dx`, but it is hidden from PE. (d) is small: SP's longest wait for `cwT` fell from 11.5 to 6.5 us.

**The fifth pair: forecast 3, measured 14.0.** This is the largest error. From 6.2 us I took `s`, the tail's waits in slots 0 to 5, and a smaller clock loss. None of this shows. PE's idle time fell from 21.0 to 11.0 us, just as in the sixth (19.2 to 9.8) and the seventh (19.8 to 10.3). The pair had the same four waits of a head as [rows 8], and gained the same. The tail's waits lie before its mark.

**The clock.** The prediction gave the second layer some 10 us of clock (1.4 at each start and 2 in each head). It gained 5.1: 4.1 in the fifth pair and 1.9 in the seventh, while the sixth and eighth lost 0.5 each. Idle time, on the other hand, was put at 8 us in the sixth and seventh pair and came to 9.4 and 9.5. Two errors of opposite sign, and the fifth pair's, make 36.9 out of 31.

**The rivals.** (4), SP's queue, was far off: DVE waited 18.9 us for rows (20.7 before, [rows 6]). (2)'s own sum, 4 x 3 + 3 x 4.2 + 2, gives 880 and not 878 us; of its 11.2 us of new waits about 5 came. (3) was refuted for the change as a whole and confirmed for the next two steps. Of the signs named, middle pairs came in just under 77 to 81 and the sixth pair at 120.1 just above 119; rows were first issued at 41.51; PE's idle time of 9.8 to 11.0 stayed well under 16.

## What to carry to other kernels

A wait is worth its length only on the engine that sets the pace of that stretch; on the engine that waits for it, moving readers apart changes nothing (first layer: 1.2 us the wrong way), while a reader with a scan queued behind it and a maker with four tiles ahead of it must be kept apart by the maker's work and not by a count of slots (second layer: 6 to 8 us a pair, for all readers moved at once). Before crediting a new order, undo its parts one at a time: here four tables of the first layer moved nothing in a middle pair, and two slots for one instruction moved 3 to 4 us. When a wait at a boundary is cured, look at once at what the next stage's first instruction needs, and when its load is issued.

## What the runs showed of the hardware

The same four DVE instructions (128x128 each, SBUF to SBUF) took 1.10, 2.19 or 3.14 us. Timelines of DVE and POOL, first `xn` in the changed kernel with one product of POOL inside its time and `xf` with POOL idle (from 147.73 on), then `xf` of the kernel with the old head, with two products:

```profile
131.27 2.19 DVE L602 TENSOR_SCALAR xn<-xt,mv,rstd 128x128 f32<-128x128 f32 x4
...
131.59 1.28 POOL L1010 TENSOR_TENSOR product<-product 128x512 f32<-128x512 f32 x1
...
147.67 1.10 DVE L602 TENSOR_SCALAR sg<-xn,mv,rstd 128x128 f32<-128x128 f32 x4
```

```profile
154.09 3.14 DVE L598 TENSOR_SCALAR sg<-xn,mv,rstd 128x128 f32<-128x128 f32 x4
...
154.25 1.30 POOL L1002 TENSOR_TENSOR product<-state,CB 128x512 f32<-128x512 f32 x1 [0.85 <-DVE state L710]
155.63 1.26 POOL L1006 TENSOR_TENSOR product<-product 128x512 f32<-128x512 f32 x1
```

Each POOL product within it adds about 1.0 us, and POOL's own 1.26 to 1.30 us do not grow. So the price is set by how many products happen to fall in, and cannot be read off one row. (Elsewhere in these traces a POOL product beside such a row took up to 1.42 us.) The Trainium skill (SBUF — State Buffer, Who interferes with whom) says that the later of the two blocks for the other's whole instruction; these three rows agree.

In a first-layer pair a lower clock can cost nothing. The second pair took 76.2 us at a granted clock of 1.00 (PE busy 65.7, idle 10.5) and again 76.2 at 0.96 (busy 68.8, idle 7.4): the slower products used up PE's waits for `lmax` and `zx`. What decides is where in the pair the clock is low. Ahead of `zx`, where DVE sets the pace, 0.93 cost nothing (46.4 us, as at 1.00). Behind it 0.95 cost 1.5 us and 0.90 cost 3.0. So a clock loss, too, has its price only where PE sets the pace.
